# A transformer block on one core: bank sums placed ahead of the fill tiles' sums on VectorE, a reordered switch of batch pairs, and four row buffers

## What is computed

```python
mod = (_silu(L0_c) @ L0_wmod).reshape(L0_c.shape[0], 6, 1, -1)
sa, ca, ga, sb, cb, gb = ...
h = _layernorm(x, axis=-1) * (1 + ca) + sa
x = x + ga * _L0_attn_ref(h, ...)
h = _layernorm(x, axis=-1) * (1 + cb) + sb
gate = jnp.einsum('bsd,hd->bsh', h, w_gate)
up = jnp.einsum('bsd,hd->bsh', h, w_up)
x = x + gb * jnp.einsum('bsh,dh->bsd', jax.nn.silu(gate) * up, w_down)
```

## Time and profile before

| | us |
|---|---|
| median of 3 runs | 1056.78 |
| lowest, highest | 1056.68, 1057.68 |
| the profiled execution, its own time | 1059.0 |
| span of the profiled execution | 1057.2 |

### The profile page before, as it was taken

One profiled execution on the slowest core, in us unless ns is written; L12 is line 12 of the kernel. 1 busy time (PEld: TensorE's weight loads), 2 busy tenths in 40 slices (PEclk: granted clock), 3 DMA queues, 4 the chain that ended last, 5 costly groups with the idle time before them and its releaser, 6 DMA issues.

```text
span 1057.2 us, 20638 instructions
## 1 busy us (share of the span) xinstructions
PE 1001.1 (95%) x7920; PEld 784.7 (74%) x7920; DVE 687.2 (65%) x1043; ACT 501.3 (47%) x891; POOL 559.1 (53%) x604
## 2 busy tenths in 40 slices
PE   7999999999998999999799899999979999999997
PEld 4676777777676888887576677778767778777775
DVE  5977377899955787777753354545577455545447
ACT  3676674435444444554554544434462344434330
POOL 1322530022025555568666455877788866657665
PEclk9999999999998999999999999999999999999999
DMA  6604336838255665755142112111131331121112
GB/s 216 196 12 135 74 81 177 244 100 215 68 140 147 136 138 119 173 129 138 60 120 80 60 41 60 40 60 40 61 104 56 120 120 60 41 60 42 40 40 80
DMA packets 158210, 106.36 MB, mean 101 GB/s; under 512 B 93984, under 2 KB 131104, under 8 KB 157984
## 3 DMA queue, kind: packets, MB, share of 16 engines
q1 hardware_dynamic: 158112, 105.04, 36.0%
HBM read 75.65 MB, written 29.36 MB: 99 GB/s over the span
## 4 chain that ended last, share of the span: by engine, by line
PE 63%; DVE 11%; POOL 8%; ACT 6%; DMA 5%; issue 5%; SPq 2%; DVEq 0%; POOLq 0%; ACTq 0%
PE ps L1464 60%; ACT t L1862 5%; DVE t L2180 3%; POOL t L2690 3%; PE ps L1472 3%; DVE t L2290 2%; DMA scrU<-t 2%; SPq L1325 1%; DVE t L2278 1%; DMA t<-scrN 1%; PE ps L1703 1%; DVE t L2390 1%; DMA t<-in_Wo 1%; DVE t L2190 1%; POOL t L2698 1%
## 5 line engine op out<-in xcount | busy, mean ns | idle before, releaser
L1464 PE MATMUL ps<-t,t 128*128 128x512 f32 (+7 forms) x7100 | 946.7, 326 | 46.8 <-ACT t L1862 14.0
L1464 PEld LDWEIGHTS ps<-t,t 128*128 128x128 f32 (+4 forms) x7100 | 731.7, 159 | 246.5 <-issue 52.2
L2180 DVE TENSOR_TENSOR t<-ps,t 128x512 f32<-128x512 f32 (+2 forms) x336 | 232.5, 706 | 227.2 <-PE ps L1464 172.9
L1862 ACT ACTIVATE t<-t 128x512 fp32r<-128x512 f32 (+11 forms) x433 | 272.7, 650 | 224.6 <-DVE t L2180 110.0
L1862 ACT ACTIVATE t<-ps 128x512 f32<-128x512 f32 (+5 forms) x250 | 138.1, 559 | 245.2 <-PE ps L1464 227.8
L2180 DVE TENSOR_TENSOR t<-t,t 128x512 fp32r<-128x512 f32 (+14 forms) x248 | 208.6, 861 | 45.8 <-ACT t L1862 34.5
L2690 POOL TENSOR_TENSOR t<-t,t 128x256 fp32r<-128x256 f32 x224 | 166.9, 781 | 108.4 <-ACT t L1862 107.5
L1862 ACT ACTIVATE t<-ps,t 128x64 f32<-128x64 f32 (+3 forms) x157 | 74.2, 534 | 29.0 <-PE ps L1472 15.8
L2290 DVE SCALAR_TENSOR_TENSOR t<-ps,t,t 128x511 f32<-128x511 f32 (+2 forms) x108 | 80.2, 747 | 3.4 <-ACT t L1862 0.5
L2698 POOL TENSOR_TENSOR t<-t,t 128x256 fp32r<-128x256 f32 x64 | 58.2, 938 | 21.0 <-ACT t L1862 20.0
L2621 POOL MEMSET t<- 128x3072 f32 x4 | 10.7, 2670 | 91.8 <-PE ps L1464 69.0
(11 more groups left out here) (60 smaller groups left out, 383.1 us busy)
## 6 DMA issues: line engine op xcount, KB each, us to landing
t<-in_wgu SPq DMA_DIRECT2D x32, 512.0 KB, 3.5
scrU<-t SPq DMA_DIRECT2D x60, 256.0 KB, 3.0
t<-scrU SPq DMA_DIRECT2D x32, 288.0 KB, 4.5
t<-in_wdn SPq DMA_DIRECT2D x32, 256.0 KB, 3.0
t<-scrU SPq DMA_DIRECT2D x32, 192.0 KB, 3.4
t<-in_W SPq DMA_DIRECT2D x19, 256.0 KB, 2.9
t<-in_x SPq DMA_DIRECT2D x16, 256.0 KB, 4.1
t<-in_wmod SPq DMA_DIRECT2D x4, 1024.0 KB, 6.5
```

The costliest lines, as they stand in the source:

```text
L1464: return e.matmul(o, l, r_, start=start, stop=stop, skip_group_check=True)
L1862: return e.activation(o, i, f, **kw)
L2180: return e.tensor_tensor(o, a, b, op)
```

## The change

At the start of the feed-forward part the low parts of the weights of half 1 (`w_low_ff(1)`) go from GpSimd, behind `t_raw`, to one VectorE instruction ahead of `split_h(0, 0)`. The row buffers become four: loads 0 to 3 are issued at once, 4 to 7 in iteration 1. In each iteration `copy_s(n, 2)` and `cadd(n, 1)` stand ahead of `down(it - 1, 0)` in the first half and of `down(it - 1, 7)` in the second. At the switch, `fh(7, 0)` goes behind the bank sum, the down weights' parts `w_high_d(7)` go from iteration 8 into iteration 7 ahead of the weight combinations, and all eight `add_0` stand behind `w_high_d(8)`. In the last iteration `w_high` stands ahead of `silu` t = 0.

```diff
     YA = [at(t_off + 2048 + n * 2048, [128, D]) for n in range(8)]
-    XR = [at(p_off + 33792, [128, D]), at(top + 111200, [128, D])]
+    XR = [at(o_, [128, D]) for o_ in (p_off + 33792, top + 111200, top + 113248, 16896)]
     X1 = [at(o_ + n * 2048, [128, D]) for o_ in (k_off, k_off + 4096, p_off + 8192, p_off) for n in range(2)]
...
 
-    def w_low_ff(m, free=()):
-        step("w_low_ff", m=m, slot=ff_raw[m][0], free=list(free) + [high_at[m]])
-        w_low_at[m] = tick("p_wl")
+    def w_low_ff(m, free=(), on="p"):
+        step("w_low_ff", m=m, slot=ff_raw[m][0], free=list(free) + [high_at[m]], on=on)
+        w_low_at[m] = tick({"p": "p_wl", "v": "v_wl"}[on])
         return w_low_at[m]
...
     done_r = [("rec_o", 16), ("v_s", 16)]
+    w_low_ff(1, [("pr_kq", 16), ("v_kd", 16)], "v")
     split_h(0, 0, [("pr_kq", 16), ("v_kd", 16)])
     t_raw(384, 512, [("a_cmod", 8)])
-    w_low_ff(1, [("pr_kq", 16), ("v_kd", 16)])
     w_load(3, 0, [w_low_at[1]])
...
     step("w_load_d", it=0, free=[("po_wo", 16), ("p_x1", 16)])
-    step("load_xf", n=0)
-    step("load_xf", n=1)
+    for n in range(4):
+        step("load_xf", n=n)
 
...
             copy_s(n, 1)
-            fh(7, 0)
             gated(7, 2)
             prod(n, 4)
             copy_s(n, 2)
             cadd(n, 1)
+            fh(7, 0)
             fh(7, 1)
             fl(7, 0)
-            w_high_d(7)
             gated(7, 3)
...
             copy_s(n, 1)
+            if last:
+                w_high(up_m(it), [("prod", 7 * (n - 1) + 7)])
             step("silu", it=it, t=0)
             prod(n, 4)
-            down(it - 1, 0)
             copy_s(n, 2)
             cadd(n, 1)
-            w_high(up_m(it), [("prod", 7 * (n - 1) + 7)])
+            down(it - 1, 0)
+            if not last:
+                w_high(up_m(it), [("prod", 7 * (n - 1) + 7)])
             step("silu", it=it, t=1)
...
                 turn_tile(4 * it - 4 + k - 1)
-                if 4 * it + k - 3 < 8:
-                    step("load_xf", n=4 * it + k - 3)
+                if it == 1:
+                    step("load_xf", n=k + 3)
             if it == 3 and k in (2, 4):
...
             step("load_xo", ks=(6, 7))
-        if it == 8:
-            for k in range(4):
-                step("add_0", k=k)
         n += 1
...
         prod(n, 4)
+        copy_s(n, 2)
+        cadd(n, 1)
         if it and not last:
             down(it - 1, 7)
-        copy_s(n, 2)
-        cadd(n, 1)
         if turn:
             split_h(1, 4, [("prod", 7 * n + 5)])
+            w_high_d(7)
         else:
             gated(it, 1)
             w_high_d(it)
             if it == 8:
-                for k in range(4, 8):
+                for k in range(8):
                     step("add_0", k=k)
...
                     all_posted(e)
-                if n >= 2:
-                    e.wait_ge(sem("norm_tr"), 8 + n - 1)
+                if n >= 4:
+                    e.wait_ge(sem("norm_tr"), 8 + n - 3)
                 for c in range(2):
                     e.wait_ge(sem(f"d_x1{c}"), posted(4 * s + 2 + c))
-                e.dma_start(XR[n % 2][:, :], scrN[b, s * 128:s * 128 + 128, :]).then_inc(sem(f"d_x{n % 2}"), 16)
+                e.dma_start(XR[n % 4][:, :], scrN[b, s * 128:s * 128 + 128, :]).then_inc(sem(f"d_x{n % 4}"), 16)
             elif kind == "load_x1":
...
                     n = st["n"]
-                    e.wait_ge(sem(f"d_x{n % 2}"), (64, 48)[n % 2] + 16 * (n // 2 + 1))
-                    src = XR[n % 2]
+                    e.wait_ge(sem(f"d_x{n % 4}"), (64, 48, 48, 48)[n % 4] + 16 * (n // 4 + 1))
+                    src = XR[n % 4]
                 for tok in st["free"]:
...
                    ALU.mult).then_inc(sem("v_xn1"), 1)
+            elif kind == "w_low_ff" and st["on"] == "v":
+                m = st["m"]
+                for tok in st["free"]:
+                    e.wait_ge(*at_least(tok))
+                tt(WGl[m % 3][:, :, :], WR[st["slot"]][:, :, :], WGh[m % 3][:, :, :].bitcast(f32),
+                   ALU.subtract).then_inc(sem("v_wl"), 1)
             elif kind == "t4":
...
                 signal(e.tensor_tensor(r_[:, 6, :], r_[:, 2, :], r_[:, 5, :], ALU.subtract), "p_ws")
-            elif kind == "w_low_ff":
+            elif kind == "w_low_ff" and st["on"] == "p":
                 m = st["m"]
...
                 e.wait_ge(sem("v_om"), k + 1)
-                e.wait_ge(sem(f"d_x{k % 2}"), (192, 176)[k % 2])
+                e.wait_ge(sem(f"d_x{k % 2}"), (160, 144)[k % 2])
                 in_order()
...
                 signal(e.tensor_tensor(YA[k][:, :], YA[k][:, :], gbB[k // 4][:, :], ALU.mult), "p_out")
-                e.wait_ge(sem(f"d_x{2 + k // 4}"), 48 + 64)
+                e.wait_ge(sem(f"d_x{2 + k // 4}"), 80 + 64)
                 in_order()
```

## The result

The changed kernel took 1049.60 us (median of 7, 1046.51 to 1053.29) where the kernel before took 1057.68 in the same runs: ratio 0.9917, 95% interval 0.9896 to 0.9939. Faster, by 0.8%. The forecast was 1045.6, within 1043 to 1048; 1049.6 lies above that and inside the wider range of 1040.8 to 1052.5. The profiled execution's own time is 1049.25 and its span 9.9 us shorter than before's.

What follows compares the result with a forecast made beforehand. TensorE, busy 95%, was taken to bound the kernel, so only its waits could be saved. -2.0 - 3.0 - 6.6 - 1.3 + 1.7 = -11.2 on 1059.0 gave 1047.8, as a median 1045.6 us; forecast 1043 to 1048, wider range 1040.8 to 1052.5.

Steps and rivals of the forecast that it cites:

- Opening, -2.0: Start of the feed-forward part: with low parts moved to VectorE, TensorE starts the last output product near 521.5, 2.0 us earlier.
- With the lock it gave 1.2: Opening: if VectorE's two low parts begin only when GpSimd's ends at 519.3, TensorE starts at 522.3, gaining 1.2 us.
- Row buffers, -3.0: Row tile loads: four buffers remove TensorE's waits of 0.72 and 2.31 us for DRAM; bounds 2.3 to 3.0.
- Bank sum first, -6.6: Each half iteration: the bank sum ahead of the running sum removes TensorE's wait for VectorE; 22 places at 0.3 us.
- The rival that the restart cost stays: Bank sums: the 0.4 us is TensorE's restart behind any semaphore, or the next thing ends as late; 1052.2 us, chance 0.10.
- the one that late running sums cost something: Fill tiles: the later running sum makes the next one wait for its bank at some 29 places; slower, chance 0.04.
- The switch, -1.3 and +1.7: Switch of pairs: TensorE leaves about 1.3 us sooner, but a low-clock spell behind new waits costs 1.7; net loss 0.4.
- can gain the 2.34 idle: Switch: GpSimd's chain gains its 2.34 us idle time and may give 1.87 back, so ends 0.5 to 0.95 sooner.
- my path: Switch: TensorE, started at 819.3, reaches `prod(19, 0)` at 831.6 and waits for GpSimd's low parts until about 834.4.
- if these last two are short: Sign of being wrong: short waits at the switch's end, for GpSimd's low parts and ScalarE's copy, forecast at some 2.8 us each.
- The clock, +1.7: Behind the switch's end: two new waits of some 2.8 us bring a low-clock spell again, costing 1.7 us; bounds 0 and 1.8.

Runs made afterwards that it cites:

- low28_on_vector: The changed kernel with the low parts of iteration 9's up weights moved from GpSimd to VectorE; 1043.70 us, ratio 0.9868 to the kernel before.
- switch_alone: The kernel before with only the edits of the switch of pairs; ratio 1.0003 to the kernel before.
- opening_by_order: The changed kernel with half 1's low parts back on GpSimd, behind the attention's last low part; ratio 0.9954 to the kernel before.
- down_parts_late: The changed kernel with the down weights' parts of iteration 7 put back into iteration 8; ratio 0.9901 to the kernel before.
- the second pair: The changed kernel, unaltered, measured again beside the follow-up kernels; ratio 0.9926 to the kernel before.
- bank_first: The kernel before with only the bank sums put ahead of the running sums; ratio 0.9936, -6.8 us.

## Why the prediction was right, and where it was off

**Opening, -2.0.** It gave 1.69. That TensorE started at 521.47 against the 521.5 forecast is in part luck, as 0.4 of the difference was there beforehand. VectorE's and GpSimd's timelines:

```profile
505.10 2.56 DVE L2180 TENSOR_TENSOR t<-t,t 128x1792 fp32r<-128x1792 f32 x1
...
517.67 3.15 DVE L2180 TENSOR_TENSOR t<-t,t 128x1024 fp32r<-128x1024 f32 x2 [1.26 <-ACT t L1862]
...
503.95 1.83 POOL L2671 TENSOR_TENSOR t<-t,t 128x768 fp32r<-128x768 f32 x1 [1.38 <-ACT t L1862]
...
516.77 1.83 POOL L2671 TENSOR_TENSOR t<-t,t 128x768 fp32r<-128x768 f32 x1 [4.98 <-ACT t L1862]
```

Both times GpSimd's instruction is under way first and takes its 1.83 in full, while VectorE's takes longer: 2.56 where the same form took 2.02 at 999.34, and two low parts end at 520.82, which is 518.60 (GpSimd's end) and nearly the 2.36 of two. The Trainium skill, page SBUF — State Buffer, section Who interferes with whom, calls the shared port an exclusive lock and says that issue order decides who blocks. These rows agree; the other way round GpSimd's 1.29 us sum took 2.87 behind VectorE's operation in low28_on_vector. My term had the two share, and came out 0.3 too large. With the lock it gave 1.2, 0.5 too small, because I had GpSimd's instruction end at 519.3; it ended at 518.60, and 518.60 + 2.36 + 0.66 = 521.62 is TensorE's start to 0.15.

**Row buffers, -3.0.** 3.5 in the changed kernel and 3.43 alone, both against a profile whose second wait of 2.31 was 1.5 longer than in two others with the same loads. Besides the two waits for DRAM some of ScalarE's waits behind them went too, which I had left in. Against those other profiles the term is 2.1 to 2.3, so I took it about 0.8 too large, and that the profile shows 3.5 is luck.

**Bank sum first, -6.6.** 2.64 and 2.63 (ten each) and four more at 0.26 make 6.3; alone -6.8 by its time. The number came out close because two errors nearly cancel: I took 22 places at 0.3, and there are 24 at 0.26. The mechanism was right for half of them. I had written that the bank sum runs "before the fill tile is even done"; in the first halves it does, but the one that I had shown is in a second half, and there it still waits for the fill tile. There the bank sum ends only 0.17 us before TensorE needs it. The rival that the restart cost stays has fallen, and so has the one that late running sums cost something: no such wait is in the rows.

**The switch, -1.3 and +1.7.** This is the term that was mis-sized: instead of 0.4 it cost 1.70, and 1.98 with the bank sum at its end taken off. My step was that GpSimd "can gain the 2.34 idle" and end 0.5 to 0.95 sooner. It ended later: its low parts for half 19 run to 826.57, 8.4 us before the 834.95 of the earlier trace rows, where the stage was entered 9.0 ahead, so 0.6 late (0.1 early in switch_alone). I had priced the moved low parts at the 4.17 of the place they came from; at the new place they overlap VectorE's and took 5.59. And of the 2.34 idle only 0.47 was gained: 1.87 remained as a wait for ScalarE. That GpSimd's chain decides at the end held, as low28_on_vector shows. The two waits there did not come as forecast: 0.50 and 2.56 instead of 2.8 each. TensorE had lost 4.4 us ahead of them (2.62, 0.47 and 1.33), which my path left out, and so came to `prod(19, 0)` at 826.12, which is 835.1 counted from the same entry as before's, and not 831.6. By my own sign ("if these last two are short") the first of them says that this path was wrong.

**The clock, +1.7.** It fell where I said in both profiles of the changed kernel. opening_by_order, with the same switch, has the spell too. But switch_alone and down_parts_late have the same two waits (0.51 and 2.56; 0.47 and 2.57) and no spell, so my "will, I think, bring such a spell again" is right only for some executions. What decides it is open; the windows show no cause.

**The total.** -2.0 - 3.0 - 6.6 + 0.4 = -11.2 against 0.38 + 1.69 + 3.5 + 6.3 - 2.0 = 9.9 of the profile. The medians say 8.1, and the second pair 8.0. Without the 0.38 that was there beforehand and the 1.2 or so by which before's own wait for rows was long, the profile has 8.3. Single executions of one kernel spread over some 7 us, so the agreement is better than one may ask. The largest miss is the switch, 0.4 against 2.0; the row buffers are next.

## What to carry to other kernels

Look on the engine that releases a wait, not on the one that waits: where it had been idle behind another wait of its own (here VectorE behind a fill tile), swapping two instructions costs nothing, and 24 times 0.26 us is most of this change. Read in the code all that the swapped instruction waits for: in half of the places it had a second wait for the same fill tile, and the new order came out just in time, by 0.17 us. Where the releasing engine is busy without a gap, a new order only moves the wait along; taking an instruction off its chain and onto an engine that is idle there gave 4.9 us for one line, 1.7 of it a clock spell that may come or not. And price a moved instruction at its new neighbours, since beside VectorE's two-input operations GpSimd's took 5.59 instead of 4.16.

## What the hardware showed

The time at which the feed-forward part begins differs by up to 3.4 us between profiles of programs that are identical up to there, so a term of 1 to 2 us must be read from one stage and not from the total. Even one stage of one profile can mislead: the same wait for a row load took 2.31 us in the kernel before and 0.82, 0.83 and 1.11 in three kernels with the same loads. And the spells of half clock vary in length and presence: at the opening 3.4 us in the changed kernel, 10 in bank_first, none in low28_on_vector. There the spell is mostly hidden: low28_on_vector is 1.5 us ahead of the changed kernel at 530.98 and level again at 559.37, as it then waits 0.93 at 543.07 for GpSimd's low parts, whose end differs by only 0.2 between the two.
